# An attention layer's sums over edges: one table of sums before, two tables (even tiles, odd tiles) after

## The chip, the cores and the metric

The kernel runs on one core of a Trainium2 chip. The metric is the device time of one execution in microseconds (us). The kernel before took 12523.31 us, the median of three runs (12512.99 to 12532.43). A difference of about 0.2% (25 us) or less can hardly be told from no change.

## The reference

Four graph layers run one after the other on 3125 nodes with 64 features and 103125 edges: a message-passing network of four rounds (L0), an attention layer (L1), another message layer (L2) and a normalised convolution (L3). After each comes a layernorm. The change is in L1:

```
k = tensor_product(x[edge_dst], edge_sh, wk, Cqk)     # per edge, 8 heads x 16
v = tensor_product(x[edge_dst], edge_sh, wv, Cv)      # per edge, 8 heads x 16
attn  = einsum('ehd,ehd->eh', q[edge_src], k)
ex    = exp(attn - segment_max(attn, edge_src)[edge_src])
denom = segment_sum(ex, edge_src)
alpha = ex / (denom[edge_src] + 1e-16)
upd   = segment_sum(v * alpha[..., None], edge_src)   # per node, 128 wide
out   = x @ W_self + upd @ W_out                      # then a normalisation over the nodes
```

The kernel divides at the end: it sums `v * ex` and `ex` per node and divides the one by the other.

## The kernel before

Edges are sorted into 832 tiles of 128 (`TILES["d"]`). All edges of one tile belong to one block of 128 nodes; there are 25 blocks (`NB`). The attention layer has a first pass (logits and values, lines 1499 to 1697, values written to `vtab` in DRAM), a stage that takes the maxima and the exponentials (1700 to 1828), a second pass that sums (1830 to 1926), and an update per node (1928 to 1983). Barriers of all engines (`join`) stand between them.

The second pass takes 8 tiles (`W`) a turn, so it has 104 turns (`G2`). What one group of 8 tiles passes through, engine by engine:

- SyncE (`sums_sp`) loads the values of the group into `v_in` (four buffers).
- VectorE (`sums_dve`, first half) writes the one-hot matrices of the 8 tiles (`ohs2`, buffers `oh` and `oh_c`, line 1895) and the products of values and exponentials (`msg1`, in the trace `amsg`, line 1899). ScalarE (`sums_act`) copies the exponentials themselves into `amsg`.
- TensorE (`sums_pe`) multiplies one-hot by message, 8 matmuls of 128x137 (line 1876). Each is float32 and stands in the trace as two MATMUL records, 16 a group. The results lie in one of two sets of PSUM banks.
- VectorE (`sums_dve`, second half) adds each 128x137 result to the rows of its block in `acc`, a table of 25 x 137 columns (line 1913). Which block it is comes from registers that are loaded by the TENSOR_LOAD of line 1236.

The functions are pipelined by `turns`: in VectorE's turn T it writes the operands of group T-1 and adds the results of group T-3, and the matmuls of group T-1 follow. A turn of VectorE is in this order: one-hots, messages, eight adds. Most turns run in a hardware loop whose body holds four of them (23 iterations, 92 turns); 12 more stand before and behind it, unrolled. Each engine works through its own queue in the written order.

These waits set the pace of the pass. One-hots and messages of group i wait until the matmuls of group i-2 have ended (`summed1`). The matmuls of group i wait for its operands and for all eight adds of group i-2 (line 1873). And each add waits for the add before it by a counter, `acc_set` (lines 1911 and 1912), since two tiles in a row may add to the same block. Per add VectorE's sequencer has four things to do in the loop: a register operation for the counter's value (ALU_OP, line 1911), the wait in a nop (EVENT_SEMAPHORE, 1912), a register operation for the block's address (FUSED_REGOPS, 1913), and the add.

After the pass `update1_dve` reads the table: the in-degree from each block's last column (line 1935), the denominators (1938), and then the quotients, which TensorE multiplies by the weights.

Of the kernel before, what the change touches and what calls it, by code (L numbers as in the profile page):

```python
# [5 lines left out]
ALU = mybir.AluOpType  # L6
# [6 lines left out]
P = 128  # L13
N = 3125
NE = 103125
NB = -(-N // P)
NPAD = NB * P
W = 8
# [36 lines left out]
AW = H * (HD + 1) + 1  # L55
# [43 lines left out]
def turns(eng, n, depth, lead, body, unroll=2):  # L99

    total = n + depth
    lead = -(-lead // unroll) * unroll
    loops = (n - 1 - lead) // unroll
    if loops < 2:
        lead, loops = total, 0
    for t in range(lead):
        body(Turn(n, unroll, t, t % unroll, True))
    if loops:
        with eng.Fori(lead // unroll, lead // unroll + loops) as r:
            for j in range(unroll):  # L110
                body(Turn(n, unroll, r, j, False))
        for t in range(lead + loops * unroll, total):
            body(Turn(n, unroll, t, t % unroll, True))


def build(nc, x_in, src_in, dst_in, ea16, ea64, ea9, L0_W_in, L0_b_in, L0_eW1, L0_eb1, L0_eW2, L0_eb2, L0_nW1,
# [3 lines left out]
    with ExitStack() as ctx:  # L120
        signals = {}

        def sig(name):
            if name not in signals:
                signals[name] = Signal(nc, ctx, name)
            return signals[name]
# [9 lines left out]
        pe, dve, act, pool, sp = nc.tensor, nc.vector, nc.scalar, nc.gpsimd, nc.sync  # L136
# [10 lines left out]
        def step(ins):  # L147

            done.at(ins)
            dve.wait_ge(done.sem, done.n)  # L150
# [1082 lines left out]
        def blocks_of(eng, o, i, tiles=W):  # L1233

            ng = tiles // PER[o]
            return nc.values_load_multi_w_load_instructions(
                blk[o][0:1, bass.ds(i * ng, ng)], engines=[eng.engine], min_val=0, max_val=NB - 1,
                skip_runtime_bounds_check_because="each counts those of the NB - 1 inner block ends that lie at or before its group")[1]
# [154 lines left out]
        def t1(name, shape, dt=F32):  # L1393
            return ctx1.enter_context(nc.sbuf_tensor(name, shape, dt))
# [132 lines left out]
        def upto(eng, name, k, s, lag=0):  # L1527

            if k.has(s, lag):
                eng.wait_ge(s1[name].sem, s1[name].n + k.i(s) + (1 - lag))  # L1530
# [296 lines left out]
        join()  # L1827
        loop3.close()

        acc = t1("acc", [P, NB * AW])  # L1830
        dve.memset(acc[:], 0.0)


        loop2 = ExitStack()
# [13 lines left out]
        acc_set = sig("part_added")  # L1848
# [3 lines left out]
        def psum_of(j, t):  # L1852
            b = 1 + 3 * j + t // 3
            return PS[:, b * 512 + t % 3 * AW:b * 512 + (t % 3 + 1) * AW]
# [35 lines left out]
        def sums_dve():  # L1890
            def turn(k):
                if k.live(1):
                    i, j, r = k.i(1), k.buf(1), k.buf(1, AHEAD)
                    upto(dve, "summed1", k, 1, 2)
                    dve.tensor_tensor(
                        ohs2[j][:], node_iota[:].unsqueeze(1).broadcast_to([P, W, P]),
                        key["d"][:, bass.ds(i * W, W)].unsqueeze(2).broadcast_to([P, W, P]), ALU.is_equal).then_inc(s1["oh1_set"].sem, 1)
                    dve.wait_ge(v_here[r].sem, v_here[r].n + k.uses(1, AHEAD) * 16)
                    dve.tensor_tensor(
                        msg1[j][:, :, 0:H * (HD + 1)].rearrange("p t (h d) -> p t h d", h=H)[:, :, :, 0:HD],  # L1900
                        v_in[r][:].rearrange("p t (h d) -> p t h d", h=H),
                        attall[:, bass.ds(i * (W * H), W * H)].rearrange("p (t h) -> p t h", h=H).unsqueeze(3).broadcast_to([P, W, H, HD]),
                        ALU.mult).then_inc(s1["msg_set"].sem, 1)
                if k.live(3):
                    i, j = k.i(3), k.buf(3)
                    upto(dve, "summed1", k, 3)
                    dve.nop(nofuse=True)
                    for t, b in enumerate(blocks_of(dve, "d", i)):
                        a = acc[:, bass.ds(b * AW, AW)]
                        if t or k.has(3, 1):  # L1910
                            dve.wait_ge(acc_set.sem, acc_set.n + i * W + t)
                            dve.nop(nofuse=True)
                        dve.tensor_tensor(a, a, psum_of(j, t), ALU.add).then_inc(acc_set.sem, 1)
            turns(dve, G2, depth2, lead2, turn, AHEAD)
# [17 lines left out]
        upd_set = sig("upd_set")  # L1932

        def update1_dve():
            dve.tensor_copy(deg[:], av[:, :, AW - 1])
            for i in range(NCH):
                a4 = av[:, i * CH:(i + 1) * CH, 0:AW - 1].rearrange("p b (h d) -> p b h d", h=H)
                step(dve.tensor_scalar(den[:].rearrange("p (b h) -> p b h", h=H), a4[:, :, :, HD], 1e-16, None, ALU.add))
                step(dve.reciprocal(den[:], den[:]))
                if i:  # L1940
                    dve.wait_ge(turned.sem, turned.n + i)
                for b in range(CH):
                    ins = dve.tensor_tensor(
                        upd[:, b * P:(b + 1) * P].rearrange("p (h d) -> p h d", h=H), a4[:, b, :, 0:HD],
                        den[:, b * H:(b + 1) * H].unsqueeze(2).broadcast_to([P, H, HD]), ALU.mult)
                ins.then_inc(upd_set.sem, 1)
                if i:
                    dve.wait_ge(product.sem, product.n + i)
                dve.tensor_copy(xcc[:], xT[:, i * CHN:(i + 1) * CHN]).then_inc(copied.sem, 1)
                dve.wait_ge(product.sem, product.n + i + 1)  # L1950
                step(dve.tensor_copy(att_o[:, i * CH:(i + 1) * CH, :], bank[2][:, 0:CH * D].rearrange("p (b f) -> p b f", f=D)))
# [19 lines left out]
        def update1_act():  # L1971
            for i in range(NCH):
# [3 lines left out]
                act.copy(updT[:], PS[:, 0:CHN]).then_inc(evicted.sem, 1)  # L1976

        update1_dve()
        update1_pe()
        update1_act()  # L1980
# [244 lines left out]
```

## Time and profile before

| | |
|---|---|
| median of 3 runs | 12523.31 us |
| the profiled execution's own time | 12525.73 us |
| its span, first to last instruction | 12523.9 us |
| mean granted TensorE clock, whole span | 0.764 of 2.4 GHz |
| busy over the span: PE, DVE, ACT, POOL | 74%, 46%, 11%, 65% |
| second pass, 9534.8 to 10166.5 us | 632 us, 5% of the span |
| in it (9549.8 to 10160.3): PE, DVE, ACT, POOL busy | 59%, 76%, 5%, 0% |

The shares over the whole span say nothing about this pass: GpSimd, the second busiest engine of the program, does nothing in it. What counts is what each engine waits for between 9535 and 10167 us. PE is the matmul engine, DVE VectorE, ACT ScalarE, SP SyncE; DVEq are records of VectorE's sequencer.

### The profile page before, as it was taken

How to read it: one execution, taken by the hardware profiler on the slowest of the kernel's cores; microseconds unless marked ns; L12 is line 12 of the kernel's file. 1: busy time of each engine (PE TensorE's matmuls, PEld its weight loads, DVE VectorE, ACT ScalarE, POOL GpSimd, SP SyncE). 2: the span in 40 equal slices, each digit the busy share in tenths (PEclk: the TensorE clock that was granted, in tenths of full speed). 3: DMA queues.
4: the chain of work that ended last, by engine and by line, in shares of the span. 5: the costliest groups of instructions: out<-in, count | busy, mean ns of one | idle time of the engine just before them, and what ended most of it. 6: DMA issues, size and time to landing. Idle time of an engine off the chain costs nothing. (4 is left out here: it accounts for less than half of the span.)

```text
span 12523.9 us, 184074 instructions
## 1 busy us (share of the span) xinstructions
PE 9274.0 (74%) x46241; PEld 7382.7 (59%) x46242; DVE 5811.6 (46%) x14093; ACT 1419.6 (11%) x2535; POOL 8101.0 (65%) x8276
## 2 busy tenths in 40 slices
PE   3777888777677767776777899999993558785333
PEld 1665444566566656665666677777763547674333
DVE  9773000344344434443444455555557754443333
ACT  0002333111111111111111000000000001110000
POOL 3777777777477747774776577776760007775776
PEclk6557889677777777777777899999995658886555
DMA  1333443222222222222222687777772212221111
GB/s 56 102 109 124 142 136 129 65 52 52 40 65 52 52 54 52 52 52 42 52 52 41 169 205 204 205 204 204 203 190 60 87 44 64 64 63 30 26 26 26
DMA packets 818891, 1141.33 MB, mean 91 GB/s; under 512 B 245286, under 2 KB 442294, under 8 KB 817332
## 3 DMA queue, kind: packets, MB, share of 16 engines
q1 hardware_dynamic: 367186, 610.56, 17.7%
q0 software_dynamic: 277888, 340.47, 13.0%
q10 hardware_dynamic: 173666, 188.57, 4.6%
q8 instruction: 60, 0.98, 0.0%
q14 instruction: 91, 0.75, 0.0%
HBM read 939.74 MB, written 199.09 MB: 91 GB/s over the span
## 5 line engine op out<-in xcount | busy, mean ns | idle before, releaser
L1086 POOL DMA_INDIRECT gx_l<-xr,gi_l x4160 | 4007.4, 963 | 2579.8 <-DVE gi_l L1170 1314.5
L1575 PE MATMUL psum<-cw,xa 128*128 128x256 f32 (+1 forms) x8320 | 2116.0, 397 | 0.0
L1575 PEld LDWEIGHTS psum<-cw,xa 128*128 128x128 f32 (+1 forms) x8320 | 1442.6, 189 | 611.7 <-issue 482.4
L1192 DVE TENSOR_TENSOR aggT_l<-aggT_l,psum 64x128 f32 x4160 | 1158.6, 279 | 865.3 <-DVE aggT_l L1192 727.7
L1243 PE MATMUL psum<-ptab,oht 128*128 x6656 | 1176.6, 351 | 378.1 <-issue 204.5
L1243 PEld LDWEIGHTS psum<-ptab,oht 128*128 128x128 f32 x6656 | 1116.0, 262 | 477.4 <-issue 476.0
L1204 DVE TENSOR_TENSOR pre_s_l<-psum,gx_l 128x512 f32<-128x512 f32 x520 | 359.6, 691 | 1988.2 <-DMA gx_l<-xr,gi_l 1929.6
L1563 POOL DMA_INDIRECT wkv<-wtab,ei x832 | 908.5, 1092 | 453.4 <-issue 364.1
L706 POOL DMA_INDIRECT slots_s<-rec_s,row_s x806 | 812.2, 1008 | 399.9 <-issue 395.7
L1556 POOL DMA_INDIRECT gx<-xr,gi x832 | 788.4, 948 | 373.4 <-issue 252.9
L2133 POOL DMA_INDIRECT gx_l<-xr,gi_l x832 | 797.1, 958 | 332.8 <-issue 237.1
L719 POOL DMA_INDIRECT slots_d<-rows_d,row_d x806 | 786.1, 975 | 245.7 <-issue 245.7
L1098 PE MATMUL psum<-ident,pre_s_l 128*128 128x128 f32 x2080 | 386.1, 315 | 700.6 <-DVE pre_s_l L1204 699.4
L1126 PE MATMUL psum<-w,h_l 128*128 128x128 f32 x4160 | 832.5, 362 | 0.0
L1126 PEld LDWEIGHTS psum<-w,h_l 128*128 128x128 f32 x4160 | 707.2, 257 | 170.7 <-issue 170.7
L1098 PEld LDWEIGHTS psum<-ident,pre_s_l 128*128 128x128 f32 x2080 | 253.2, 158 | 808.8 <-issue 808.8
L1137 PE MATMUL psum<-oh,msg_l 128*64 128x128 f32 x4160 | 726.4, 348 | 0.0
L1137 PEld LDWEIGHTS psum<-oh,msg_l 128*64 128x64 f32 x4160 | 657.0, 184 | 49.8 <-issue 40.0
L1642 DVE TENSOR_TENSOR xa<-oh,shb 128x512 f32<-128x512 f32 (+1 forms) x1040 | 661.4, 684 | 10.8 <-issue 6.1
L1161 ACT ACTIVATE msg_l<-psum 128x512 f32<-128x512 f32 x520 | 310.5, 597 | 2600.6 <-PE psum L1126 2600.6
L1137 PE MATMUL psum<-oh_b_l,msg_l 128*64 128x128 f32 x4160 | 590.8, 303 | 1.0 <-DVE oh_b_l L1181 1.0
L1149 ACT ACTIVATE h_l<-psum 128x512 f32<-128x512 f32 x520 | 310.5, 597 | 2169.2 <-PE psum L1098 2166.2
(341 smaller groups left out, 11934.1 us busy)
## 6 DMA issues: line engine op xcount, KB each, us to landing
shb<-shT SPq DMA_DIRECT2D x1872, 128.0 KB
kr<-keyrow_s SPq DMA_DIRECT2D x416, 256.0 KB
gx_l<-xr,gi_l POOLq DMA_INDIRECT x4992
wtab<-eo ACTq DMA_DIRECT2D x152, 512.0 KB, 4.0
vtab<-kv ACTq DMA_DIRECT2D x208, 256.0 KB, 2.4
v_in<-vtab SPq DMA_DIRECT2D x104, 512.0 KB, 3.3
hT<-noderow SPq DMA_DIRECT2D x101, 512.0 KB
kr<-keyrow_d SPq DMA_DIRECT2D x208, 128.0 KB
```

Source lines behind the costliest of these rows:

```text
L706: scattered[j].at(pool.indirect_dma_start(slots["s"], bass.IndirectOffsetOnAxis(ap=row["s"][:, c:c + 1], axis=0), rec_s[:, c, :], None, bo ...
L719: gone_d[j].at(pool.indirect_dma_start(slots["d"], bass.IndirectOffsetOnAxis(ap=row["d"][:, g * FC + c:g * FC + c + 1], axis=0), rows_d[:, ...
L1086: pool.indirect_dma_start(gx[j][:, c_, :], None, xr, bass.IndirectOffsetOnAxis(ap=gi[j][:, c_:c_ + 1], axis=0)).then_inc(rows_in[j].sem, 16)
L1126: ins = pe.matmul(bank[2][:, q * P:(q + 1) * P], h1[:, q * P:(q + 1) * P], w2[:], start=False, stop=True, skip_group_check=True)
L1137: ins = pe.matmul(sums(j, t // per), msg[j][:, t * D:(t + 1) * D], ohs[j][:, t, :], start=t % per == 0, stop=(t + 1) % per == 0)
L1192: ins = dve.tensor_tensor(a, a, sums(j, h), ALU.add)
L1243: ins = pe.matmul(bank[0][:, t * D:(t + 1) * D], oht[:, t * P:(t + 1) * P], ptab[:, bass.ds(bl[t // PER["s"]] * D, D)], start=True, stop=True)
L1556: pool.indirect_dma_start(gx2[j][:, t, :], None, xr2, bass.IndirectOffsetOnAxis(ap=gi1[j][:, t:t + 1], axis=0)).then_inc(rows_in1[j].sem, 16)
L1563: pool.indirect_dma_start(wkv[j][:, t, :], None, wtab, bass.IndirectOffsetOnAxis(ap=ei1[j][:, t:t + 1], axis=0)).then_inc(wrows_in[j].sem, 16)
L1575: ins = pe.matmul(bank[2 + p][:, t % 2 * OKV:(t % 2 + 1) * OKV], xa[j][0:n_, c, t * P:(t + 1) * P], cw[0:n_, c, :], start=c == 0, stop=c = ...
L1642: ins = dve.tensor_tensor(xa[j][0:n_, c, :], xT2[j][0:n_, :], shb[j][0:n_, c, :], ALU.mult)
L2133: pool.indirect_dma_start(gx[j][:, c_, :], None, xr, bass.IndirectOffsetOnAxis(ap=gi[j][:, c_:c_ + 1], axis=0)).then_inc(rows_in3[j].sem, 16)
```

## The change

Two tables, `acc` and `acc_odd`, are cleared before the pass. Within a group of eight, tiles 0, 2, 4, 6 add to `acc`, tiles 1, 3, 5, 7 to `acc_odd`. Each add waits for the add before the last, the one that wrote the same table. In front of the update the second table is added to the first, and the update waits for that.

```
-        acc = t1("acc", [P, NB * AW])
+        acc, acc_odd = t1("acc", [P, NB * AW]), t1("acc_odd", [P, NB * AW])
         dve.memset(acc[:], 0.0)
+        dve.memset(acc_odd[:], 0.0)
...
                     for t, b in enumerate(blocks_of(dve, "d", i)):
-                        a = acc[:, bass.ds(b * AW, AW)]
-                        if t or k.has(3, 1):
-                            dve.wait_ge(acc_set.sem, acc_set.n + i * W + t)
+                        a = (acc, acc_odd)[t % 2][:, bass.ds(b * AW, AW)]
+                        if t >= 2 or k.has(3, 1):
+                            dve.wait_ge(acc_set.sem, acc_set.n + i * W + t - 1)
                             dve.nop(nofuse=True)
                         dve.tensor_tensor(a, a, psum_of(j, t), ALU.add).then_inc(acc_set.sem, 1)
...
         def update1_dve():
+            step(dve.tensor_tensor(acc[:], acc[:], acc_odd[:], ALU.add))
             dve.tensor_copy(deg[:], av[:, :, AW - 1])
```

VectorE's queue at the start of the pass, before: the clearing of the table and of the message buffers, and the first one-hots.

```order
2363 L1831 MEMSET acc 128x3425 [waits barrier_Pool_Activation_PE_DVE_SP_release]
2364 L1843 MEMSET amsg0 128x1096
2365 L1843 MEMSET amsg1 128x1096
2366 L1895 TENSOR_TENSOR oh<-node_iota,key_d 128x1024 [waits barrier_Pool_Activation_PE_DVE_SP_release]
2367 L1899 TENSOR_TENSOR amsg0<-v_in0,attall 128x8x8x16 [waits s_v_here0]
```

The same place now.

```order
2363 L1831 MEMSET acc 128x3425 [waits barrier_Pool_Activation_PE_DVE_SP_release]
2364 L1832 MEMSET acc_odd 128x3425
2365 L1844 MEMSET amsg0 128x1096
2366 L1844 MEMSET amsg1 128x1096
2367 L1896 TENSOR_TENSOR oh<-node_iota,key_d 128x1024 [waits barrier_Pool_Activation_PE_DVE_SP_release]
2368 L1900 TENSOR_TENSOR amsg0<-v_in0,attall 128x8x8x16 [waits s_v_here0]
```

One MEMSET of 3425 columns is in front of the barrier that opens the pass.

The adds of a group in VectorE's queue, before (the first of the group that is the first to be added; ISA rows are the sequencer's register operations, and `s_part_added` is the counter `acc_set`).

```order
2373 L1913 ISA
2374 L1913 TENSOR_TENSOR acc<-acc,psum 128x137
2375 L1913 ISA [waits s_part_added]
2376 L1913 TENSOR_TENSOR acc<-acc,psum 128x137
2377 L1913 ISA [waits s_part_added]
```

The same adds now.

```order
2374 L1914 ISA
2375 L1914 TENSOR_TENSOR acc<-acc,psum 128x137
2376 L1914 ISA
2377 L1914 TENSOR_TENSOR acc_odd<-acc_odd,psum 128x137
2378 L1914 ISA [waits s_part_added]
2379 L1914 TENSOR_TENSOR acc<-acc,psum 128x137
```

The number of adds, of waits (but for one) and of register operations is the same. The tables alternate, and each wait asks for a count lower by one. No instruction moves past another in the queues of TensorE, ScalarE, SyncE or GpSimd.

## Rows read from the trace of the kernel before

**Rows 1.** Busy time by stretch: the second pass.

```profile
core 0: us, PE busy (x) PEld busy (x) DVE busy (x) ACT busy (x) POOL busy (x), PEclk, DMA share, GB/s
...
9549.80:10160.30 610.50, 361.00 (x1630) 334.98 (x1631) 463.75 (x1014) 30.27 (x100) 0.00 (x0) 0.63 0.26 83
```

**Rows 2.** Groups by line, 9535 to 10167 us: count, busy us, mean ns, idle before.

```profile
L1913 DVE TENSOR_TENSOR acc<-acc,psum 128x137 f32 x832 | 246.9, 297 | 144.2 <-DVE acc L1913 144.2
L1876 PE MATMUL psum<-amsg,oh_c 128*128 128x137 f32 x832 | 190.2, 416 | 137.5 <-DVE acc L1913 137.5
...
L1899 DVE TENSOR_TENSOR amsg<-v_in,attall 128x1024 f32<-128x1024 f32 x104 | 126.7, 1219 | 2.1 <-DMA v_in<-vtab 2.1
L1895 DVE TENSOR_TENSOR oh_c<-node_iota,key_d 128x1024 f32<-128x1024 f32 x52 | 63.5, 1221 | 6.5 <-issue 6.5
```

**Rows 3.** Timeline of one turn: start, length, engine, line, idle time before.

```profile
9802.35 0.30 DVE L1913 TENSOR_TENSOR acc<-acc,psum 128x137 f32 x1 [0.20 <-DVE acc L1913]
9802.56 1.22 DVE L1895 TENSOR_TENSOR oh_c<-node_iota,key_d 128x1024 f32<-128x1024 f32 x1
...
9802.79 2.72 PE L1876 MATMUL psum<-amsg,oh 128*128 128x137 f32 x16 [2.35 <-DVE acc L1913]
9803.70 1.22 DVE L1899 TENSOR_TENSOR amsg<-v_in,attall 128x1024 f32<-128x1024 f32 x1
9804.83 0.29 DVE L1913 TENSOR_TENSOR acc<-acc,psum 128x137 f32 x1
...
9805.32 0.30 DVE L1913 TENSOR_TENSOR acc<-acc,psum 128x137 f32 x1 [0.20 <-DVE acc L1913]
...
9808.27 0.30 DVE L1913 TENSOR_TENSOR acc<-acc,psum 128x137 f32 x1 [0.20 <-DVE acc L1913]
9808.49 1.22 DVE L1895 TENSOR_TENSOR oh<-node_iota,key_d 128x1024 f32<-128x1024 f32 x1
```

**Rows 4.** The sequencer's part of an add, lines 1913 and 1912, ns min/median/max.

```profile
L1913 DVEq FUSED_REGOPS  x832: 57/57/71, 9544.2 to 10166.1; - x167
...
L1912 DVEq EVENT_SEMAPHORE  x831: 21/21/21, 9546.1 to 10166.0; - x167
```

**Rows 5.** Line 1911 between 9803.4 and 9803.9 us: first and last start.

```profile
L1911 DVEq ALU_OP  x2: 40/40/40, 9803.5 to 9803.7; - x2
```

**Rows 6.** Timeline of the attention's maxima: dependent small operations without registers.

```profile
9484.91 0.16 DVE L1773 TENSOR_TENSOR ctmp<-ctmp,oht 1x8 f32<-1x8 f32 x1
...
9490.93 0.16 DVE L1774 TENSOR_TENSOR oht<-ctmp,oht 1x8 f32<-1x8 f32 x1
```

**Rows 7.** Timeline of TensorE and VectorE as the pass fills.

```profile
9539.45 3.99 PE L1876 MATMUL psum<-amsg,oh 128*128 128x137 f32 x16 [20.87 <-DVE amsg L1899]
...
9543.48 1.23 DVE L1895 TENSOR_TENSOR oh<-node_iota,key_d 128x1024 f32<-128x1024 f32 x1 [1.86 <-PE psum L1876]
```

**Rows 8.** Busy time by stretch (columns as in Rows 1): two groups of matmuls.

```profile
9573.78:9575.90 2.12, 2.11 (x16) 1.91 (x16) 2.12 (x2) 0.00 (x0) 0.00 (x0) 1.00 0.00 0
9652.25:9656.24 3.99, 3.99 (x16) 3.67 (x16) 3.23 (x6) 0.00 (x0) 0.00 (x0) 0.50 0.17 31
```

**Rows 9.** Timeline at the opening of the pass: the clearing.

```profile
9529.33 2.91 DVE L1831 MEMSET acc<- 128x3425 f32 x1 [7.12 <-PEq L141]
9532.42 0.97 DVE L1843 MEMSET amsg<- 128x1096 f32 x1 [0.17 <-issue]
```

**Rows 10.** Line 409, an addition of two SBUF tensors, ns min/median/max.

```profile
L409 DVE TENSOR_TENSOR rank<-rank,member x13: 998/999/1000, 59.0 to 146.4; 128x806 f32<-128x806 f32 x13
```

**Rows 11.** Timeline behind the pass: last add, first operations of the update.

```profile
10166.20 0.30 DVE L1913 TENSOR_TENSOR acc<-acc,psum 128x137 f32 x1 [0.20 <-DVE acc L1913]
10166.82 0.18 DVE L1935 COPY deg<-acc 128x25 f32<-128x25 f32 x1 [0.33 <-PEq L141]
```

**Rows 12.** Loads of the values, 9540 to 10160 us: count, size, time to landing.

```profile
v_in<-vtab SPq DMA_DIRECT2D x99, 512.0 KB, 3.3
```

## The prediction

> **What bounds the kernel now.** The page of the whole span does not decide here, so I first cut out the second pass with the busy times by stretch: VectorE is busy 464 of 610 us, TensorE 361, ScalarE 30, GpSimd 0, and the granted clock is 0.63 [rows 1]. Next the groups by line, with what ended the idle time before each. TensorE's idle time ends with the last add of a group (137.5 us before one buffer's matmuls, the other's are alike), and VectorE's own idle time before the adds, 144.2 us, ends with the add before: it waits for itself [rows 2]. The values' loads land in 3.3 us and are issued up to four turns ahead; only the first was waited for, 2.1 us [rows 2, 12].
>
> Then one turn in the timeline [rows 3]. From one-hot (9802.56) to the next one-hot (9808.49) is 5.93 us, and VectorE's pieces fill it: 1.14 us to the messages (9803.70), 1.13 to the first add (9804.83), 3.44 from the first to the eighth add (9808.27), 0.22 to the next one-hot. Nothing else intervenes, so VectorE's queue is the bound and the eight adds are 3.44 + 0.22 = 3.66 us of it. An add takes 0.297 us, but the next one starts 0.49 us after it (3.44 over 7 gaps is 0.491): 0.20 us is lost from the end of one to the start of the next. Where no wait separates two operations they overlap: the one-hot starts 0.21 us after the last add's start, 0.09 before that add has ended.
>
> **The change part by part.** *The loosened wait.* Three things limit how close adds can stand once each waits for the one before the last.
> (a) The datapath: 0.21 us, the add to one-hot spacing [rows 3].
> (b) The wait itself: the same-table chain still needs 0.49 us for two adds, 0.247 us each.
> (c) The sequencer. The 0.197 us from the end of an add to the next start hold more than the semaphore. In the maxima stage 31 steps of dependent operations of 0.16 us take 9490.93 - 9484.91 = 6.02 us, 0.194 each, so a wait on a finished operation costs only 0.035 us where no register is needed [rows 6]. The other 0.16 us is issue: the wait's record of 21 ns, the register operation of 57 ns [rows 4], and the gaps between them. In front comes the ALU_OP of 40 ns [rows 5], today hidden beside the running add; with its gaps I put it at 0.11 us. Together 0.27 us an add. The trace shows this loop once a turn, where the sequencer runs ahead beneath the messages and nothing holds it: its first two ALU_OPs start at 9803.5 and 9803.7, rounded, so 0.1 to 0.3 us apart [rows 5], which has room for 0.27 and does not prove it. The extremes are (a) and no gain at all, 0.49.
>
> I take 0.27, the largest of the three. The first two adds of a turn are issued ahead, beneath the messages. Add 2 waits for add 0, 0.49 us after it, as add 1 does today; add 1 slips in between at 0.21. Adds 3 to 7 follow at 0.27 each: 0.49 + 5 x 0.27 = 1.84 us in place of 3.44. A turn saves 1.60 us and falls from 5.93 to 4.33; 104 turns save 166.4 us. The 6.5 us at the loop's 23 branches [rows 2] stay: the sequencer then has nothing issued ahead, today or after.
>
> The page "VectorE: DVE Perf Modes" of the Trainium skill speaks against the change. Its section on the DRAIN that can't be avoided says the next operation does not start until the pipe is empty, that leaving semaphores out of a chain gained nothing, and its rules for authors say to cut operations and not semaphores. By that the sum would have no gain, only the two added operations. The rows disagree where an independent operation follows (0.21 us against 0.297 us), and the same section grants that an operation that is not held starts earlier.
>
> *What is late next.* TensorE. In a turn now, its group starts 0.23 us after VectorE's turn has ended (9802.79 against 9802.56) [rows 3] and takes 3.99 us where the granted clock is 0.50, that is 1.2 GHz, and 2.12 us at 1.00, 2.4 GHz [rows 8]. The circle that could bind is over two turns: one-hots wait for the matmuls of two groups earlier, those started at the end of a turn of VectorE, after its adds. So two turns must last at least one turn of VectorE (4.33), 0.23, the matmuls (3.99), and the way back, 0.04 us where no register is involved (9543.44 to 9543.48 [rows 7]) plus some 0.17 for the register operation that carries the wait: 8.76 us, or 4.38 a turn, if every group ran at 1.2 GHz. VectorE needs 4.33, and 4.42 averaged with the branches, whose extra 0.37 us or so every fourth turn makes room. At most about 0.11 us in four turns is left exposed, 3 us in the pass; since part of the groups has the faster clock I charge 1 us. The cover of the matmuls is thus nearly used up, but not gone.
>
> On the clock: in this pass the granted value averages 0.63 while the matmuls are busy 59% of the time [rows 1]; after the change they would be busy some 80%. "TensorE: Matmul & The Clock Gate" of the Trainium skill, in its part on the warm-up, says that sustained activity brings 2.4 GHz; by that rule TensorE's circle falls away entirely and the 1 us with it. No row here shows this pass at a denser load.
>
> ScalarE's copies wait for the same matmuls and are 0.30 us long, far from the bound. The loads of 512 KB would come every 4.4 us instead of 6.0 at 83 GB/s [rows 1], some 114 GB/s; the landing of 3.3 us is hidden by the four buffers.
>
> *The second clearing.* From the first MEMSET's start to the next one is 3.09 us (9529.33 to 9532.42) [rows 9]. Everybody waits at the barrier: +3.1 us, all exposed.
>
> *The final addition.* 3425 columns, two SBUF inputs. Line 409 takes 0.999 us for 806 columns and the messages 1.219 for 1024 [rows 10, 2]; between these two the slope is 1.01 ns a column, from the larger 1.219 + 2401 x 1.01 = 3.64, and in proportion to columns 4.08 at most. I take 3.7, plus 0.035 for its wait. It stands between the last add and the copy of the degrees, on VectorE, which starts at once after the barrier [rows 11], with all engines idle: +3.7 us.
>
> *The sum*: -166.4 + 1 + 3.1 + 3.7 = -158.6 us. Against the profiled execution's own 12525.73 us this gives 12367; that execution lies 2.4 us above the median, so 12365 us in the terms of the median, 1.27% faster. A difference below 0.2%, 25 us, could not be told from none.
>
> **The rivals.**
> *Closer adds.* If the sequencer's loop is shorter than I think, the same-table chain binds: adds at 0, 0.21, 0.49, 0.70, 0.98, 1.19, 1.47, 1.68, a turn of 4.17, a saving of 1.76 x 104 = 183 us less 6.8, so 12347. For it: twelve turns are unrolled and have no ALU_OP. Against it: the issue work counted above, and that TensorE at 1.2 GHz then holds two turns to 4.17 + 0.23 + 3.99 + 0.21 = 8.60, 4.30 a turn, above 4.17; 12350 to 12360 is then likelier than 12347.
>
> *Adds that stretch each other.* An add reads PSUM, and reads and writes SBUF, while the one before still writes; if that, or a longer issue, puts them 0.35 us apart, a turn saves 3.44 - 0.49 - 5 x 0.35 = 1.20 us, 125 in all, net 118: 12405. The overlap of add and one-hot, with the one-hot's usual 1.22 us [rows 3], speaks against it, though there the second reads no PSUM.
>
> *No overlap at all, slower than before.* If an add cannot start before the one ahead has ended and reported it, each gap stays at 0.49 us and the kernel pays the clearing and the final addition: +6.8 us, 12530. Its place is the 7 gaps of a turn; it decides as soon as the mean gap shrinks by less than 6.8 us / 728 = 9 ns. Against it stands the 0.21 us spacing. The Trainium skill's section on the DRAIN, named above, is the rule that would bring this about.
>
> *The change does nothing of what it says* would need both tables' adds to wait on the same count; the waits differ by one, and the first group's second add has none.
>
> **How the numbers follow.** My forecast 0.70 (alone 12355 to 12380), closer adds 0.10, stretching adds 0.12, no overlap 0.06, something else that costs 0.02. The range takes in the first three: 12345 to 12405. Faster by over 0.2%: 0.92. Within 0.2%: 0.07, which is the no-overlap case (its 6.8 us are too few to be told) and a little more. Slower by more: 0.01.
>
> **What would show it.** In the profile after, the idle time before the adds should fall from 144 us to near zero, while their count and 297 ns stay. The timeline of a turn should show starts at about 0, 0.21, 0.49, then every 0.27, and one-hots every 4.33 us. VectorE should be busy all through the pass, its busy time even above the elapsed share since records overlap, and the pass should end some 165 us earlier after its start. TensorE's idle time per group should shrink to about 0.4 us at 1.2 GHz, its clock be equal or higher. An idle time "released by the matmuls" before one-hots, of more than some 10 us in total, would say that TensorE took over; a mean gap of 0.49 that there is no overlap; one above 0.30 that I have the issue or the datapath wrong. The prediction is also wrong if any stage outside 9525 to 10175 us moves by more than a few us.

## The result and the profile after

The changed kernel took 12369.24 us (median of 4 runs, 12359.80 to 12373.06), the kernel before in the same comparison 12527.87 us. The ratio is 0.9874, with a 95% interval of 0.9856 to 0.9891: 1.3% faster. The prediction was 12365 us, by a difference of -158.6 us; the medians differ by 158.6. Measured again on another occasion, the same kernel gave 0.9881 (0.9864 to 0.9897), against 12506.75 us.

The profiled execution took 12365.76 us with a span of 12364.0. First the groups by line in the second pass (count, busy us, mean ns, idle before), to be set beside [rows 2].

```profile
L1877 PE MATMUL psum<-amsg,oh_c 128*128 128x137 f32 x832 | 147.7, 346 | 92.2 <-DVE acc_odd L1914 92.2
...
L1914 DVE TENSOR_TENSOR acc<-acc,psum 128x137 f32 x416 | 123.3, 296 | 4.1 <-DVE acc_odd L1914 2.2
L1914 DVE TENSOR_TENSOR acc_odd<-acc_odd,psum 128x137 f32 x416 | 123.0, 296 | 0.0
L1896 DVE TENSOR_TENSOR oh_c<-node_iota,key_d 128x1024 f32<-128x1024 f32 x52 | 63.5, 1222 | 6.5 <-issue 6.5
L1896 DVE TENSOR_TENSOR oh<-node_iota,key_d 128x1024 f32<-128x1024 f32 x52 | 63.4, 1219 | 2.2 <-PE psum L1877 1.9 <-PEq L141 0.3
...
L1936 DVE TENSOR_TENSOR acc<-acc,acc_odd 128x3425 f32<-128x3425 f32 x1 | 3.7, 3728 | 0.3 <-PEq L141 0.3
```

There are as many adds as before, 832, and one still takes 296 ns. What is gone is the idle time in front of them: 144.2 us before, 4.1 now. The one-hots wait for the matmuls once, 1.9 us while the pass fills, as before, and once more for 0.05 us (the turn that starts at 9576.74); TensorE did not become the bound. TensorE still waits for the adds, 92.2 us in front of one buffer where it was 137.5: 1.8 us a group, not the 0.4 us that the prediction names for 1.2 GHz, since most groups were shorter than 3.99 us (below).

One turn in the timeline (start, length, engine, line), which answers to [rows 3]:

```profile
9803.46 1.22 DVE L1896 TENSOR_TENSOR oh<-node_iota,key_d 128x1024 f32<-128x1024 f32 x1
9804.60 1.22 DVE L1900 TENSOR_TENSOR amsg<-v_in,attall 128x1024 f32<-128x1024 f32 x1
9805.74 0.29 DVE L1914 TENSOR_TENSOR acc<-acc,psum 128x137 f32 x1
9805.94 0.29 DVE L1914 TENSOR_TENSOR acc_odd<-acc_odd,psum 128x137 f32 x1
9806.22 0.30 DVE L1914 TENSOR_TENSOR acc<-acc,psum 128x137 f32 x1
9806.49 0.30 DVE L1914 TENSOR_TENSOR acc_odd<-acc_odd,psum 128x137 f32 x1
9806.76 0.30 DVE L1914 TENSOR_TENSOR acc<-acc,psum 128x137 f32 x1
9807.03 0.30 DVE L1914 TENSOR_TENSOR acc_odd<-acc_odd,psum 128x137 f32 x1
9807.30 0.30 DVE L1914 TENSOR_TENSOR acc<-acc,psum 128x137 f32 x1
9807.57 0.30 DVE L1914 TENSOR_TENSOR acc_odd<-acc_odd,psum 128x137 f32 x1
9807.78 1.22 DVE L1896 TENSOR_TENSOR oh_c<-node_iota,key_d 128x1024 f32<-128x1024 f32 x1
```

The adds start 0, 0.20, 0.48, 0.75, 1.02, 1.29, 1.56 and 1.83 us after the first, and the turn lasts 9807.78 - 9803.46 = 4.32 us. An add now begins while the one before is still running (0.27 us apart, 0.30 long), so the lengths overlap.

The ends of the pass: the second clearing, and the final addition.

```profile
9528.36 2.91 DVE L1831 MEMSET acc<- 128x3425 f32 x1 [7.12 <-PEq L141]
9531.94 2.91 DVE L1832 MEMSET acc_odd<- 128x3425 f32 x1 [0.66 <-issue]
...
9535.03 0.97 DVE L1844 MEMSET amsg<- 128x1096 f32 x1 [0.17 <-issue]
```

```profile
10002.82 0.29 DVE L1914 TENSOR_TENSOR acc_odd<-acc_odd,psum 128x137 f32 x1
10003.44 3.73 DVE L1936 TENSOR_TENSOR acc<-acc,acc_odd 128x3425 f32<-128x3425 f32 x1 [0.33 <-PEq L141]
10007.20 0.18 DVE L1937 COPY deg<-acc 128x25 f32<-128x25 f32 x1
```

From the first clearing to the degrees' copy it is 10007.20 - 9528.36 = 478.84 us; before it was 10166.82 - 9529.33 = 637.49 [rows 9, 11]. The difference is 158.65 us. What lies outside hardly moved, as the prediction asked: the part in front of the clearing is 1.0 us shorter (9528.36 against 9529.33 us), the part behind the degrees' copy 0.3 us (2356.8 against 2357.1 us).

The same 400 us of both kernels, busy time by stretch (columns as in [rows 1]), first before, then after:

```profile
9560.00:9960.00 400.00, 232.81 (x1060) 215.88 (x1060) 304.30 (x665) 20.28 (x67) 0.00 (x0) 0.64 0.27 88
```

```profile
9560.00:9960.00 400.00, 252.69 (x1448) 233.16 (x1448) 391.60 (x901) 27.27 (x90) 0.00 (x0) 0.80 0.37 118
```

VectorE went from 76% to 98% busy, the loads from 88 to 118 GB/s, and the granted clock from 0.64 to 0.80. TensorE did 1448 matmul records in place of 1060 while its busy time rose only from 233 to 253 us.

### The profile page after: what moved, and what is told of

It is laid out like the page before. It is cut to its first block and busy times, and to the rows that moved or that the text cites. A ratio compares the mean times of both kernels' runs of the same rounds, so it can differ in the third digit from the quotient of the medians.

```text
span 12364.0 us, 184075 instructions
## 1 busy us (share of the span) xinstructions
PE 9193.0 (74%) x46241; PEld 7304.0 (59%) x46242; DVE 5788.1 (47%) x14095; ACT 1419.9 (11%) x2535; POOL 8100.3 (66%) x8276
```

## The experiments

The runs were made on three more occasions, each with the kernel before beside them (12511.32, 12506.75 and 12517.32 us), so their medians are compared by ratio. Since single terms are a few us and runs of one kernel differ by 10 to 40, each kernel also has a stretch from its profile: from the start of the first clearing on VectorE to the start of the first reduction of the normalisation behind the update. Turn means are of 103 one-hot to one-hot steps in the trace. Three rows are the kernel after and two the kernel before, as the text explains: their stretches agree within 2.1 and 0.8 us.

```
kernel                              median us  ratio (95% interval)      stretch us    mean turn us
before                              12527.87   1                         692.4         5.99
after                               12369.24   0.9874 (0.9856-0.9891)    533.7         4.43
after, again                        12361.60   0.9881 (0.9864-0.9897)    534.0         4.43
two tables, old wait                12524.57   1.0008 (0.9999-1.0018)    707.8         6.06
after, empty instruction            12351.26   0.9873 (0.9857-0.9890)    535.8         4.43
before, empty instruction           12515.62   1.0004 (0.9995-1.0014)    693.2         6.00
after, one more wait behind an add  12403.99   0.9909 (0.9892-0.9925)    572.2         4.78
before, one more wait behind an add 12515.84   1.0003 (0.9994-1.0013)    699.8         6.06
after, adds of 64 columns           12334.89   0.9859 (0.9843-0.9876)    521.0         4.31
after, matmuls twice                12361.65   0.9879 (0.9863-0.9894)    539.7         4.47
three tables                        12348.61   0.9875 (0.9859-0.9892)    518.7         4.21
four tables                         12325.45   0.9851 (0.9834-0.9867)    502.6         3.99
four tables, three waits a group    12329.98   0.9860 (0.9844-0.9877)    503.7         4.00
four tables, cheaper ends           12314.45   0.9832 (0.9819-0.9846)    488.0         4.00
```

**The changed kernel again**, as the yardstick for the kernels with more tables.

> The changed kernel once more, as the yardstick for the kernels with more tables on the same chip: ratio to before 0.987.

It gave 0.9881, and a stretch of 534.0 us against 533.7: stretches repeat far better than whole runs.

**The tables without the loosened wait.**

```
-                        if t >= 2 or k.has(3, 1):
-                            dve.wait_ge(acc_set.sem, acc_set.n + i * W + t - 1)
+                        if t or k.has(3, 1):
+                            dve.wait_ge(acc_set.sem, acc_set.n + i * W + t)
```

> Both tables, both clearings and the final addition, but each add waits again for the add just before it. My theory (the gain is the loosened wait alone): start to start of two adds 0.49 us as before, the stretch from first clearing to the update 6.8 us longer than before, time about 12535 us. Rival (the two tables themselves spread the accesses and so let the adds come closer): spacing clearly below 0.49 us and a time well below 12528 us.

The ratio is 1.0008 (0.9999 to 1.0018), some 10 us more and not to be told from no change by the runs alone, and the adds stand 0.49 us apart as before:

```profile
9805.02 0.30 DVE L1914 TENSOR_TENSOR acc<-acc,psum 128x137 f32 x1 [0.20 <-DVE acc_odd L1914]
9805.52 0.30 DVE L1914 TENSOR_TENSOR acc_odd<-acc_odd,psum 128x137 f32 x1 [0.20 <-DVE acc L1914]
...
9813.09 0.30 DVE L1914 TENSOR_TENSOR acc_odd<-acc_odd,psum 128x137 f32 x1 [0.32 <-DVE acc L1914]
```

So two tables by themselves bring nothing closer, and the whole gain is the wait's. The stretch grew by 15.5 us, not 6.8. The pass itself is 7.6 us longer, and most of that comes from the loop, whose rounds of four turns last 24.40 us in place of 24.10: twice in each round a step of the sequencer takes some 0.12 to 0.16 us more. The last row shows one of the two, 0.32 us idle in place of 0.20; the other is at the loop's branch. Each falls on the same instruction in every round. The kernel before has such a step too, between an add and the ALU_OP behind it (0.139 us in place of 0.025), where the running add hides it. Here, with one instruction more ahead of the loop, it falls between the address's register operation and the add (0.228 in place of 0.104). That it is the fetching of instructions, and that the shifted position is its reason, is my reading and was not tested.

**An empty instruction behind each add**, in the kernel after and in that before: `dve.nop(nofuse=True)`.

> The changed kernel with one more empty instruction of VectorE's sequencer behind each add. Theory (the sequencer's loop of 0.27 us bounds adds 3 to 7): each of these gaps and the one to the next one-hot grows by some 0.05 us, 0.27 to 0.32, six a turn, 92 turns in the loop: about +29 us, 12398. Rival (the wait for the same table's add, or the datapath, bounds them): the empty instruction is hidden, 0.27 stays, +0 to 5 us, 12369 to 12374.

> The kernel before with the same empty instruction behind each add. Theory: it runs beside the 0.30 us add that the next one waits for, so the 0.49 us spacing stays and only the step to the one-hot grows by 0.05 us a turn: about +5 us, 12533. Rival (an instruction of the sequencer always costs its time): 8 x 0.05 x 104 = +42 us, 12570.

Nothing changed in either, and neither theory gains by it. The traces have no record of the instruction: VectorE's records of the pass are as many, kind by kind, as without it. Without a wait it left nothing in the queue, and the two runs are repetitions of the kernels after and before. The experiment was then made with an instruction that stays, a wait for a count reached long ago:

```
                         dve.tensor_tensor(a, a, psum_of(j, t), ALU.add).then_inc(acc_set.sem, 1)
+                        dve.wait_ge(done.sem, done.n)
+                        dve.nop(nofuse=True)
```

> The changed kernel with one more wait of VectorE's sequencer behind each add, on a count that was reached long ago (an empty instruction without a wait left nothing in the queue). Theory (sequencer bound): adds 3 to 7 start every 0.32 in place of 0.27 us and the step to the one-hot grows by 0.05, some +0.3 us a turn, +29 us in all. Rival (same-table chain or datapath bound): hidden, 0.27 stays.

> The kernel before with the same extra wait behind each add. Theory: hidden beside the running add in 7 of 8 places, spacing 0.49 us as before, at most +0.05 us a turn, +5 us. Rival (the sequencer's instructions always add): +42 us.

In the changed kernel:

```profile
9803.53 0.30 DVE L1914 TENSOR_TENSOR acc<-acc,psum 128x137 f32 x1
9803.87 0.30 DVE L1914 TENSOR_TENSOR acc_odd<-acc_odd,psum 128x137 f32 x1
9804.21 0.30 DVE L1914 TENSOR_TENSOR acc<-acc,psum 128x137 f32 x1
```

The spacing is 0.34 us in place of 0.27, +38 us in the stretch (29 expected). In the kernel before the same instruction leaves the spacing at 0.49 and costs 7.4 us in the stretch, less than a run can tell:

```profile
9803.76 0.30 DVE L1913 TENSOR_TENSOR acc<-acc,psum 128x137 f32 x1 [0.20 <-DVE acc L1913]
9804.25 0.30 DVE L1913 TENSOR_TENSOR acc<-acc,psum 128x137 f32 x1 [0.20 <-DVE acc L1913]
```

Between adds that wait for each other the same edit is free; in the five gaps where they no longer do it is paid in full. That is what the sequencer's loop as the new bound means. The size was off: 0.068 us an instruction, not 0.05. The 7.4 us come mostly from rounds of 24.38 us in place of 24.10, in which the branch and one stalled step are 0.12 to 0.14 us longer, as with the old wait above.

The trace of the changed kernel shows the loop itself. From one add's start it is 0.025 us to the next ALU_OP, 0.088 on to the wait's record, 0.053 to the register operation and 0.104 to the next add: 0.270 us, with every count reached before it was asked for. The same step can be found in the trace before. The two ALU_OPs of [rows 5], where nothing holds the sequencer, start at 9803.452 and 9803.722 when they are not rounded, 0.270 us apart.

**Adds of 64 columns in place of 137** (73 columns of the sums left out).

```
-dve.tensor_tensor(a, a, psum_of(j, t), ALU.add)
+dve.tensor_tensor(a[:, 0:64], a[:, 0:64], psum_of(j, t)[:, 0:64], ALU.add)
```

> The changed kernel, but each add covers 64 of its 137 columns (the other 73 columns of the sums are left out), so an add is 0.076 us shorter. Theory (sequencer bound): adds 3 to 7 still start every 0.27 us; add 1 comes up to 0.08 us earlier, without use, and add 2, which waits for add 0, 0.08 earlier: -0.08 us a turn, -8 us, about 12361. Rival (datapath bound): 0.076 x 8 x 104 = -63 us, 12306.

```profile
9802.29 0.22 DVE L1914 TENSOR_TENSOR acc<-acc,psum 128x64 f32 x1
9802.42 0.22 DVE L1914 TENSOR_TENSOR acc_odd<-acc_odd,psum 128x64 f32 x1
9802.70 0.22 DVE L1914 TENSOR_TENSOR acc<-acc,psum 128x64 f32 x1
9802.97 0.22 DVE L1914 TENSOR_TENSOR acc_odd<-acc_odd,psum 128x64 f32 x1
9803.24 0.22 DVE L1914 TENSOR_TENSOR acc<-acc,psum 128x64 f32 x1
```

The adds are 0.22 us long, and from the third on still start every 0.27 us, now with a gap between them. More than halving the columns of an add saved 12.7 us of the stretch where a datapath bound would have given 63. Had the same-table chain set the pace, it would show too: the third add now comes 0.41 us after the first in place of 0.48, yet the later spacing stayed. The pair that was issued ahead came closer, 0.13 us, which is the datapath's part of an add of 64 columns, and so did the step from the last add to the one-hot, 0.16 us in place of 0.21; the expectation of 8 us had left that out.

**Three and four tables.** Three: tile t adds to table t mod 3. Four: t mod 4; for room the second one-hot buffer then lies in an idle one.

```
three: dve.wait_ge(acc_set.sem, acc_set.n + i * W + max(t - 2, 0))
four:  dve.wait_ge(acc_set.sem, acc_set.n + i * W + t - 3)
```

> Three tables, tile t of a group to table t mod 3; adds 0 to 2 wait only for the group before, add t from 3 on for add t-2's predecessor, the last one to its own table. Theory (adds 3 to 7 run at the sequencer's 0.27 us, because the wait of add 2 for add 0 uses up the lead that the sequencer has built beneath the messages): the wait of add 3 for add 0 costs nothing now and part of the lead is kept, adds at 0, 0.21, 0.41, 0.62, 0.83, 1.04, 1.30, 1.57 us, a turn of 4.05 in place of 4.32: -28 us, and one more clearing and final addition +6.9: about 21 us below the changed kernel, 12348. Rival (the sequencer's loop of 0.27 holds from the second add on whatever the tables): no gain in the turns, +6.9 us, 12376. Second rival (the same-table chain of 0.49 us for two adds was the limit): all adds at 0.21.

> Four tables, each add waits for the one four before; the second one-hot buffer takes the place of the idle transposed one-hots, for room. Theory (lead kept): the wait of add 4 for add 0 is over before its slot, issue stays ahead, all adds start 0.21 us apart, a turn of 3.93 us: -40 us in the pass, two more clearings and final additions +13.7, so about 26 us below the changed kernel, 12343. Rival (sequencer's loop binds from the second add): +13.7 us, 12383. Rival (TensorE, at 1.2 GHz two turns need 3.93 + 0.23 + 3.99 + 0.21 us): turns of 4.18 and idle time of the one-hots released by the matmuls.

Three tables, then four (eight adds merged to a row: the first one's start, and the time they cover):

```profile
9801.55 1.22 DVE L1897 TENSOR_TENSOR oh_c<-node_iota,key_d 128x1024 f32<-128x1024 f32 x1
...
9801.77 3.99 PE L1878 MATMUL psum<-amsg,oh 128*128 128x137 f32 x16 [1.13 <-DVE acc L1915]
...
9803.82 1.86 DVE L1915 TENSOR_TENSOR acc<-acc,psum 128x137 f32 x8
...
9805.93 1.22 DVE L1897 TENSOR_TENSOR oh<-node_iota,key_d 128x1024 f32<-128x1024 f32 x1 [0.26 <-PE psum L1878]
```

```profile
9802.71 1.74 DVE L1915 TENSOR_TENSOR acc<-acc,psum 128x137 f32 x8
9804.36 1.22 DVE L1897 TENSOR_TENSOR oh<-node_iota,key_d 128x1024 f32<-128x1024 f32 x1
```

With three tables the starts in the loop are 0.21 us apart up to the sixth add and 0.26 and 0.27 at the end; turns of 4.05 us, as expected. With four, all are 0.21 us apart and the one-hot follows the first add by 1.65 us; turns of 3.93 us. Against the yardstick the stretch fell by 15.3 and 31.4 us (expected 21 and 26). The rival in which the sequencer's 0.27 us holds whatever the tables is wrong: its loop is the same in these kernels, but it is ahead. What costs the changed kernel its lead is add 2's wait for add 0.

What the three-table kernel lacks to the forecast is TensorE. Its pass became 22.0 us shorter, not 28, and 19 of its turns ended late, 5.6 us in all, because the one-hot waited for a group of matmuls, most of them at 1.2 GHz. The rows show such a turn: the group ends at 9805.76, the one-hot starts 0.17 us later, and the turn lasts 4.38 us. This is the circle of two turns that the prediction describes: 4.05 + 0.23 + 3.99 + 0.17 = 8.44 us, and from 9797.49 to 9805.93 it is 8.44. With four tables no one-hot in the loop waited for a group, and no group there took longer than 3.41 us. The stall of the sequencer (0.11 us in one turn of four with three tables) is hidden with four, and the branch of the loop cost 0.21 us a round where it had cost 0.37.

**Four tables with three waits a group** in place of eight.

> Four tables as before, but a group has three waits in place of eight: add 0 for the group before, add 4 for adds 0 and 1, add 6 for adds 0 to 3. Theory: the five waits left out were hidden by the sequencer's lead already, so as four tables, 3.93 us a turn, 0 to 5 us less since an occasional stall of the sequencer is covered better. Rival (each wait costs its issue time): 5 x 0.05 us or more a turn, 26 us below four tables.

The stretch is 503.7 against 502.6 us: no difference. Here the waits that the lead already hid were not worth removing.

**Every matmul twice.**

> The changed kernel with every matmul of the pass issued twice into the same place: a group takes 4.24 us at 2.4 GHz, 7.98 at 1.2. Theory (TensorE's circle: two turns last at least a turn of VectorE, 0.23, the group and 0.21 us): at 2.4 GHz 2T >= 4.32 + 0.23 + 4.24 + 0.21 = 9.00, four turns 18.0 in place of 17.77 us, about +6 us and the clock near full speed; were it at 1.2 GHz, turns of 8 us and +370 us. Rival (TensorE binds as soon as its group is as long as VectorE's turn, by its work alone): 4.24 is below 4.32, no change at all.

The stretch grew by 5.7 us and the mean turn by 0.04. The group took less than I had put: from 9800.69 to the end of the last record, 9804.67, 3.98 us, since matmuls overlap. The way back from there to the one-hot was 0.17 us. With both the circle gives 4.32 + 0.23 + 3.98 + 0.17 = 8.70 us for two turns, and the two turns without a branch or stall are 4.38 + 4.32 = 8.70. So TensorE sets the pace of one turn in four, against the rival of no change at all. That the total met the +6 us of the expectation is chance, though. Four turns went from 17.77 to 17.83 us, not to 18.0, some 1.4 us in 23 rounds; 1.65 us come from the filling of the pass, where the first one-hot that waits for a group waits 3.5 us in place of 1.9, and the rest from the unrolled turns at both ends. The clock:

```profile
9560.00:9960.00 400.00, 357.99 (x2879) 342.47 (x2880) 391.38 (x897) 27.00 (x89) 0.00 (x0) 1.00 0.40 118
```

**The best version**, four tables with cheaper ends.

```
+        for x in tabs[2:]:
+            pool.memset(x[:], 0.0)
...
+            def whole(i):
+                c = slice(i * CH * AW, (i + 1) * CH * AW)
+                for x in tabs[1:]:
+                    step(dve.tensor_tensor(acc[:, c], acc[:, c], x[:, c], ALU.add))
```

> Four tables as before, with cheaper ends: GpSimd, idle here, clears two of the four while VectorE clears the others, and the three final additions go block by block, the first fifth in front of the update, the rest while VectorE waits for TensorE in it. Theory: both ends stood exposed; clearing costs 2 x 3.09 us less, the additions 3 x 3.76 become 3 x 0.9 exposed: 15 us below four tables, ratio to before 0.984. Rival: GpSimd clears slower than VectorE and the opening gets longer, or the additions delay VectorE's part of the update: no gain.

```profile
9536.45 5.84 POOL L1835 MEMSET acc<- 128x3425 f32 x2 [171.93 <-POOLq L141]
9537.24 2.91 DVE L1833 MEMSET acc<- 128x3425 f32 x1 [7.12 <-PEq L141]
...
9967.42 2.69 DVE L1942 TENSOR_TENSOR acc<-acc 128x685 f32<-128x685 f32 x3 [0.33 <-PEq L141]
9970.14 0.22 DVE L1947 TENSOR_SCALAR den<-acc 128x40 f32<-128x40 f32 x1
```

GpSimd clears its two tables (5.84 us) beside VectorE's, and 2.7 us of additions stand in front of the update in place of three whole ones. The stretch is 488.0 us, 14.6 below four tables (expected 15), and the ratio 0.9832 (0.9819 to 0.9846) is the lowest of all, though it was measured on another occasion than 0.9851.

## Why the prediction was right

**What bounds the pass.** VectorE waiting for itself, as read from [rows 2, 3]: the wait loosened, the idle time went, and the stages outside moved by 1.3 us in all. The tables alone gave none of it.

**The spacing of the adds.** The starts came out at 0.20, 0.48 and then every 0.27 us, against 0.21, 0.49 and 0.27, and the turn at 4.32 against 4.33. The reason held too. Of the three limits, the sequencer's binds: an instruction more in it lengthens the spacing, less work in the add does not shorten it, and keeping its lead (four tables) removes it. The prediction put 0.11 us in front of the wait and 0.16 behind it by estimate; the trace has 0.025 + 0.088 and 0.053 + 0.104. The same-table chain of 0.247 us was near enough to be mistaken for it; the one more wait and the 64 columns tell them apart.

**The sum.** From the first one-hot to the last the pass went from 616.8 to 455.9 us, 160.9 less, and the adds-only turns at its end and what else lies before the final addition gave 5.1 more: 166.0 against 166.4 forecast. Within that, two small things cancel. One turn in four is 4.44 us: a step of the sequencer, 0.11 us longer than the others, which the running add hid before, is now exposed in each of 23 rounds, 2.5 us. And the 12 unrolled turns, which have no ALU_OP, alternate 0.21 and 0.28 us and last 4.17, 0.16 us less than forecast. The clearing cost 3.58 us (3.1 forecast; 0.66 us of idle time stands in front of it, which [rows 9] could not show for a second MEMSET of that size), the final addition 3.76 (3.7). In all 158.65 us.

**TensorE.** I charged 1 us for it; it cost 0.05. Its granted clock in the 400 us was 0.64 before, 0.80 now, 0.97 with four tables, 1.00 with every matmul twice. Of the 104 groups of matmuls 6 took 2.12 us (2.4 GHz) before and 49 now, and 38 took some 3.99 us (1.2 GHz) before and 5 now. "TensorE: Matmul & The Clock Gate" of the Trainium skill, part on the warm-up, says that sustained activity brings 2.4 GHz; the trace agrees in direction, but at 0.80 not the whole way. Nor was TensorE busy 80% of the time, as I put it, but 63%, since the groups got shorter. The circle of two turns is right in form: the kernel with three tables fell into it at 1.2 GHz, and the doubled matmuls did at 2.4. Its way back is 0.17 us, not 0.04 + 0.17, so at 1.2 GHz it gives 8.72 us for the changed kernel in place of 8.76; the two turns in front of the one late one-hot took 8.69.

**The rivals.** No overlap: refuted by the starts. The section "The DRAIN you can't avoid" in "VectorE: DVE Perf Modes" of the Trainium skill, read as a rule for this case, would have given it; here an add begins 0.21 us after another of 0.30 us where it need not wait, and the loosened waits of 832 adds gave back 166 us. Stretching adds: the mean length stayed at 296 ns and the spacing at 0.27 us, not 0.35. Closer adds came true only in the unrolled turns.

**Where luck had a part.** The change moved the loop's code, and such a shift can cost: in the kernel with the old wait it cost some 7 us that no step of mine held. Here it was 2.5 us and was balanced by the unrolled turns. That the medians differ by the very 158.6 us of the forecast is chance: the interval of the ratio spans 137 to 180 us. What supports the size is the stretch, 158.7 us shorter in one profile and 158.4 in the other.

## What to carry to other kernels

Where an engine's idle time ends with its own last instruction, look at what that wait protects. If it is one accumulator, a second copy lets two adds share one dependent step (0.49 us here), for one more clearing and one addition at the end. Then ask what is next: here the sequencer, whose register operations and waits per add (0.27 us) were longer than the add's own 0.21. It cost nothing as long as it was ahead, so place the first wait that really waits late enough (four tables) that the lead built beneath long operations is kept, and put the one-off costs on idle engines. Then ask again what is next: at turns of 4.05 us it was TensorE.

## What the runs showed that I had not expected

- An added wait of the sequencer that is met at once cost 0.068 us where exposed and left the spacing at 0.49 us where a dependent wait covered it.
- A stall of 0.11 to 0.16 us returned at fixed instructions of the loop, once or twice in a round of four turns. Which instruction it hit, and so whether it was hidden, differed between kernels whose queues differ by one or two instructions. Its cause was not tested.
- GpSimd cleared 3425 float32 columns in 2.95 us by the profile, whose spans of GpSimd are rough, VectorE in 2.91.
